# Causal attention's relative-position transfers: shorter rows for the upper 64 partitions, and the triangle filled by GpSimd selects instead of TensorE mask products

## The reference

```python
QEr = jnp.einsum('bhsd,ld->bhsl', q, Er_s)
Srel = _skew(QEr)                 # row s is shifted so that column t holds Er of distance s - t
QK = jnp.einsum('bhsd,bhtd->bhst', q, k)
attn = (QK + Srel) / math.sqrt(dh)
attn = jnp.where(tril, attn, -jnp.inf)
attn = softmax(attn); out = attn @ v
```

## Time and profile before

| | |
|---|---|
| three executions | 1282.5, 1283.88, 1286.7 us |
| the profiled execution | 1286.1 us |
| its span, first to last instruction | 1284.6 us |
| mean granted TensorE clock | 0.91 |
| busy: TensorE, VectorE, ScalarE, GpSimd | 1011.8, 696.2, 647.5, 223.0 us |
| causal attention, first load issued to last score | about 81 to 385 us |

### The profile page before, as it was taken

One profiled execution on the slowest core, in us unless ns is written; L12 is line 12 of the kernel. 1 busy time (PEld: TensorE's weight loads), 2 busy tenths in 40 slices (PEclk: granted clock), 3 DMA queues, 4 the chain that ended last, 5 costly groups with the idle time before them and its releaser, 6 DMA issues. The chain is left out here.

```text
span 1284.6 us, 22764 instructions
## 1 busy us (share of the span) xinstructions
PE 1011.8 (79%) x6434; PEld 632.7 (49%) x6435; DVE 696.2 (54%) x2140; ACT 647.5 (50%) x1346; POOL 223.0 (17%) x531
## 2 busy tenths in 40 slices
PE   5746778788783746999999993355899999997487
PEld 3414444455452425999999992121333333334344
DVE  4735778888887621010101101475766666684597
ACT  2435777777772212333232331143677777763787
POOL 0000000000000360111111112701222222240232
PEclk9865999999996877999999997576999999998799
DMA  7478889999998657665666641345211111110001
GB/s 247 149 258 307 321 329 337 344 341 339 337 324 329 237 180 240 189 214 185 208 196 195 208 147 50 103 157 155 63 47 46 47 44 48 44 38 9 1 29 39
DMA packets 93319, 227.41 MB, mean 177 GB/s; under 512 B 9686, under 2 KB 51766, under 8 KB 87254
## 3 DMA queue, kind: packets, MB, share of 16 engines
q1 hardware_dynamic: 86454, 208.20, 46.5%
q0 software_dynamic: 6816, 18.62, 5.3%
HBM read 143.07 MB, written 83.62 MB: 176 GB/s over the span
## 5 line engine op out<-in xcount | busy, mean ns | idle before, releaser
L684 DVE CUSTOM_DVE_ANT_0 unused<-mpsS,mask_bias 128x512 bf16<-128x512 f32 x256 | 172.0, 691 | 82.8 <-PE mpsS L617 82.7
L711 ACT ACTIVATE mPT<-mpsB 128x512 f32<-128x512 f32 x256 | 152.6, 597 | 80.0 <-PE mpsB L624 73.7
L1358 ACT ACTIVATE hT<-ph,w 128x128 f32<-128x128 f32 x312 | 89.0, 368 | 198.0 <-PE ph L1332 198.0
L464 PE MATMUL psT<-ident,scores 128*128 128x128 f32 x640 | 108.6, 286 | 58.0 <-ACT scores L557 56.1
L1377 DVE TENSOR_TENSOR ys<-py,b 128x256 f32<-128x256 f32 x39 | 16.6, 425 | 249.3 <-PE py L1342 249.3
L512 DVE CUSTOM_DVE_ANT_0 scores<-psS,bias 128x512 f32<-128x512 f32 (+3 forms) x256 | 119.7, 487 | 53.1 <-DMA bias<-rel 45.1
L1332 PE MATMUL ph<-xT,w 128*128 128x128 f32 x1248 | 146.8, 276 | 0.0
L552 ACT COPY stage<-psE 128x512 f32<-128x512 f32 (+1 forms) x192 | 97.5, 510 | 97.6 <-DMA rel<-stage 70.8
L1332 PEld LDWEIGHTS ph<-xT,w 128*128 128x128 f32 x1248 | 143.7, 193 | 0.1
L1342 PE MATMUL py<-w,hT 128*128 x624 | 141.2, 379 | 0.7 <-DVE ys L1377 0.7
L557 ACT ACTIVATE scores<-scores,nm 128x128 f32<-128x128 f32 (+3 forms) x256 | 136.8, 566 | 5.2 <-DVE nm L525 5.2
(11 more groups left out here) (247 smaller groups left out, 1482.5 us busy)
## 6 DMA issues: line engine op xcount, KB each, us to landing
rel<-stage SPq DMA_DIRECT2D x64, 640.0 KB, 6.7
bias<-rel SPq DMA_DIRECT2D x64, 640.0 KB, 7.2
w<-in_w1p SPq DMA_DIRECT2D x39, 1028.0 KB
qk<-packed SPq DMA_DIRECT2D x64, 192.0 KB
mqk<-packed SPq DMA_DIRECT2D x64, 192.0 KB
w<-in_w2p SPq DMA_DIRECT2D x8, 1024.0 KB
slots_in<-zero_row SPq DMA_DIRECT2D x1, 4992.0 KB, 18.2
xs<-slots_in SPq DMA_DIRECT2D x39, 128.0 KB
```

The costliest lines, as they stand in the source:

```text
L464: tr = nc.tensor.transpose(psT[bank][:, to:to + P], scores[slot][:, at:at + P], ident[:, :])
L684: nc.vector.tensor_tensor_reduce(out=unused[:, i, :], in0=psS[i % 2][:, :], in1=mask_bias[:, i, :], scale=1.0, scalar=-3.0e38, op0=ALU.add ...
L711: nc.scalar.activation(PT[r][:, j, :], psB[j % 2][:, :], ACT.Exp, scale=1.0 / 4).then_inc(s_exp, 1)
```

## The change

The columns of `stage` and `rel` are laid out anew: tile 1 at 0, tile 2 at 256, tile 0 at 640, tile 3 at 768, so that two segments of 640 columns (`SEG`) each begin with a tile. The row pitch of `rel` becomes 1281 elements (5124 bytes), and column 1280 of `stage` holds -2^100 from the start. For every head GpSimd runs two `affine_select` instructions on `stage`, each over 2 x 128 columns of 128 rows: of each tile's first 128 columns, row p keeps those from column 127 - p on and gets -2^100 below. After the skew these elements stand above the diagonal of the neighbouring tile, so the mask products are gone. In rows 0 to 63 the first 64 columns of both segments would always be -2^100. They are set once, in DRAM (in the opening) and in `bias`, and are left out of both transfers. So each write and each read becomes two DMAs: rows 64 to 127 whole, and rows 0 to 63 as two pieces of 576 columns (2304 bytes) each.

```diff
+UNIT_AT = [768, 256, 0]
+TRIM = P // 2
+SEG = 640
...
+    REL_P = REL_W + 1
+    rel = [dram(f"rel_{r}", (P, REL_P), F32) for r in range(RING)]
...
@@ SP
-                            sp.wait_ge(s_wr[slot], 16 * (turn + 1))
+                            sp.wait_ge(s_wr[slot], 32 * (turn + 1))
...
-                            skewed = bass.AP(rel[slot].ap().tensor, P - 1, [[REL_W - 1, P], [1, REL_W]])
-                            sp.dma_start(bias[slot][:, :], skewed).then_inc(s_rd[slot], 16)
+                            rel_t = rel[slot].ap().tensor
+                            if isinstance(n, int) and n == -READ:
+                                sp.wait_ge(s_blank_bias, RING)
+                            sp.dma_start(bias[slot][TRIM:P, :], bass.AP(rel_t, P - 1 + TRIM * (REL_P - 1), [[REL_P - 1, P - TRIM], [1, REL_W]])
+                                         ).then_inc(s_rd[slot], 16)
+                            sp.dma_start(bias[slot][0:TRIM, :].rearrange("p (g c) -> p g c", c=SEG)[:, :, 0:SEG - TRIM],
+                                         bass.AP(rel_t, P - 1, [[REL_P - 1, TRIM], [SEG, 2], [1, SEG - TRIM]])).then_inc(s_rd[slot], 16)
...
-                            sp.wait_ge(s_eev, NU * (m + 1))
-                            wait(sp, s_rd[slot], 16 * turn)
-                            sp.dma_start(rel[slot][:, :], stage[slot % 2][:, :]).then_inc(s_wr[slot], 16)
+                            sp.wait_ge(s_cut, 2 * (m + 1))
+                            if isinstance(n, int) and n == -REL:
+                                sp.wait_ge(s_edge, 2)
+                            wait(sp, s_rd[slot], 32 * turn)
+                            sp.dma_start(rel[slot][TRIM:P, :], stage[slot % 2][TRIM:P, :]).then_inc(s_wr[slot], 16)
+                            sp.dma_start(bass.AP(rel[slot].ap().tensor, TRIM, [[REL_P, TRIM], [SEG, 2], [1, SEG - TRIM]]),
+                                         stage[slot % 2][0:TRIM, 0:REL_W].rearrange("p (g c) -> p g c", c=SEG)[:, :, TRIM:SEG]).then_inc(s_wr[slot], 16)
@@ TensorE
-                            nc.tensor.matmul(psS[bank][:, off:off + w], q_k[:, i * P:(i + 1) * P],
-                                             q_k[:, S:S + w], start=True, stop=False)
-
-                            mm = nc.tensor.matmul(psS[bank][:, off + w - P:off + w], identb[:, :], dmask[:, :],
-                                                  start=False, stop=True)
+                            mm = nc.tensor.matmul(psS[bank][:, off:off + w], q_k[:, i * P:(i + 1) * P],
+                                                  q_k[:, S:S + w], start=True, stop=True)
@@ VectorE, ahead of its loop
+                    for rows in stage:
+                        nc.vector.memset(rows[:, REL_W:REL_P], NEG).then_inc(s_edge, 1)
+                    for r in range(RING):
+                        nc.vector.memset(bias[r][0:TRIM, :], NEG).then_inc(s_blank_bias, 1)
@@ GpSimd
-                    pool.wait_ge(vals.s_zero, 3)
+                    keep = dict(base=-(P - 1), channel_multiplier=1, compare_op=ALU.is_ge, fill=nc.gpsimd.to_reg(NEG))
...
+                        if h := stage_of(n, r, it, REL):
+                            m, slot, turn = h
+                            rows = stage[slot % 2]
+                            pool.wait_ge(s_eev, NU * (m + 1))
+                            pool.sem_inc(s_seen_pool, 1)
+                            for first in (rows[:, 0:2 * SEG].rearrange("p (u c) -> p u c", c=SEG)[:, :, 0:P],
+                                          rows[:, 256:1280].rearrange("p (u c) -> p u c", c=512)[:, :, 0:P]):
+                                nc.gpsimd.affine_select(out=first, in_=first, pattern=[[0, 2], [1, P]], **keep).then_inc(s_cut, 1)
+                        if isinstance(n, int) and n == 0:
+                            pool.wait_ge(vals.s_zero, 3)
...
-                    run_heads(pool, 0, NBH - 1, step)
+                    run_heads(pool, -LOAD, NBH - 1, step)
@@ ScalarE
-                                nc.scalar.copy(stage[slot % 2][:, 512 * i:512 * i + WU[i]],
+                                nc.scalar.copy(stage[slot % 2][:, UNIT_AT[i]:UNIT_AT[i] + WU[i]],
@@ opening, SP, between the load of above and the wait on s_es
+                        sp.wait_ge(s_blank, 1)
+                        for r in range(RING):
+                            sp.dma_start(bass.AP(rel[r].ap().tensor, 0, [[REL_P, TRIM], [SEG, 2], [1, TRIM]]),
+                                         blank[:, :, :]).then_inc(s_blank, 16)
+                            sp.dma_start(bass.AP(rel[r].ap().tensor, REL_W - 1, [[REL_P, TRIM], [1, 2]]), blank[:, 0, 0:2]).then_inc(s_blank, 16)
```

More of the change, by code:

```diff
@@ L64, in build @@
     slots_out = dram("slots_out", (SLOT_TILES * P, D), F32)
-    rel = [dram(f"rel_{r}", (P, REL_W), F32) for r in range(RING)]
+    REL_P = REL_W + 1
+    rel = [dram(f"rel_{r}", (P, REL_P), F32) for r in range(RING)]
     with top:
@@ L82, in build @@
         s_const = sem("s_const")
+        s_blank = sem("s_blank")
         s_ctx = [sem(f"s_ctx{i}") for i in range(2)]
@@ L384, in causal_attention @@
             WU = [u[-1][1] + u[-1][2] for u in units]
-            place = {i: (512 * u + off, w) for u, unit in enumerate(units) for i, off, w in unit}
+            place = {i: (UNIT_AT[u] + off, w) for u, unit in enumerate(units) for i, off, w in unit}
             key_place = {j: (512 * u + off, w) for u, unit in enumerate(CAUSAL_KEYS) for j, off, w in unit}
@@ L390, in causal_attention @@
                 qk = [sb(ctx, f"qk{r}", [KP, 2 * S], BF16) for r in range(ROUND)]
-                stage = [sb(ctx, f"stage{r}", [P, REL_W]) for r in range(2)]
+                stage = [sb(ctx, f"stage{r}", [P, REL_P]) for r in range(2)]
                 bias = [sb(ctx, f"bias{r}", [P, REL_W]) for r in range(RING)]
@@ L403, in causal_attention @@
                 s_rd = [sem(f"s_rd{r}") for r in range(RING)]
-                names = ("emm", "eev", "smm", "soft", "nm", "exp", "tmm", "tev", "seen", "seensp")
-                s_emm, s_eev, s_smm, s_soft, s_nm, s_exp, s_tmm, s_tev, s_seen, s_seen_sp = (
+                s_blank_bias = sem("s_blank_bias")
+                names = ("emm", "eev", "smm", "soft", "nm", "exp", "tmm", "tev", "seen", "seensp", "cut", "edge", "seenpool")
+                s_emm, s_eev, s_smm, s_soft, s_nm, s_exp, s_tmm, s_tev, s_seen, s_seen_sp, s_cut, s_edge, s_seen_pool = (
                     sem(f"s_{n}") for n in names)
@@ L502, in step @@
                             m, slot, turn = soft
-                            dve.wait_ge(s_rd[slot], 16 * (turn + 1))
+                            dve.wait_ge(s_rd[slot], 32 * (turn + 1))
                             wait(dve, s_tmm, NU * (m - RING + 1))
@@ L510, in step @@
                                 for i, off, w in unit:
-                                    at = 512 * u + off
+                                    at = UNIT_AT[u] + off
                                     ttr = nc.vector.tensor_tensor_reduce(
@@ L543, in step @@
                         if early and (not isinstance(n, int) or early[0] >= 2):
-                            act.wait_ge(s_wr[(r + REL - 2) % RING], 16 * (it * (ROUND // RING) + (r + REL - 2) // RING + 1))
+                            act.wait_ge(s_wr[(r + REL - 2) % RING], 32 * (it * (ROUND // RING) + (r + REL - 2) // RING + 1))
                         if soft:
@@ L734, in opening @@
                     above = sb(c1, "above", [P, P])
+                    blank = sb(c1, "blank", [TRIM, 2, TRIM])
                     s_er, s_above, s_cc, s_es, s_pick = (sem(f"s_{n}") for n in ("er", "above", "cc", "es", "pick"))
@@ L764, in _ @@
                         sp.wait_ge(s_pick, 16 * PIECES)
+                        sp.wait_ge(s_blank, 16 * 2 * RING + 1)
                         k.stored(sp)
@@ L801, in _ @@
                         nc.vector.memset(zero_row[:, :], 0.0).then_inc(s_cc, 1)
+                        nc.vector.memset(blank[:, :, :], NEG).then_inc(s_blank, 1)
                         nc.vector.memset(V[:, :, :, DH:VW], 1.0).then_inc(s_cc, 1)
```

## The result

The changed kernel takes **1345.8 us** (median of four runs, 1343.4 to 1347.4) and the kernel before, on the same chip, 1284.2: ratio **1.0477**, 95% interval 1.0453 to 1.0501. That is 62 us slower (57 us between the two profiled executions, 1343.4 and 1286.1). The forecast was 3 us faster; the sign is that of rival A, which gave 1361.

The account below looks back on a forecast made before the run. Six DMA engines were taken to bound the stage at 98%. Pace -4.2, mask products at half clock -1.0 and start +1.8 gave -3.4 us: 1280.5 us from the median 1283.9, range 1275 to 1380 (own range 1275 to 1287).

Parts of the forecast that it names:

- rival A: rel transfers touching only 64 partitions run at half rate: 5.8 us a head, some 1361 us, up to 1380; chance 0.33.
- the price of the shorter transfers: rel writes and reads: smaller packets cut the six engines' time to 4.30 us a head, 0.07 to 0.09 less.
- Six engines as the bound: DMA queue: qk loads of 96 rows sit on six engines, which bound the stage at 98%, 4.37 us for 4.47 measured.
- what is late next: Behind the transfers stands the compute loop waiting for TensorE's product, floor 4.34 us; pace taken as 4.39, 4.2 us less.
- This loop keeps its length: Compute loop of TensorE and ScalarE: removing the mask products leaves its 4.34 us unchanged.
- Mask products at pace, nothing: TensorE: their 51.7 us are busy time of an engine that waits anyway, so removing them gains nothing at pace.
- Rival B: Something small eats the gain: odd-pitch rows, selects over 2.1 us, or a later TensorE clock rise; together 0.15, 1285 to 1325.
- The microsecond at half clock: TensorE at 1.2 GHz: without mask products 0.32 us a head over three heads, 1.0 us less (0 to 2).
- Selects: GpSimd, two a head at 0.5 us each (0.3 to 1.5); they delay the write but cost nothing at pace.
- Row pitch: Part of the second rival: writes to 5124-byte rows could cost 10 ns or more a packet, 0 to +5 us.
- SP's issues: SP: two more DMA issues a head at 0.33 us each, 2.1 us of 4.4 in all, hidden by the queue's line.
- Start: Head 0, before the first score: selects, handing over and second issues add 1.8 us (1 to 3).

Follow-up runs that it names:

- before_spread: The kernel before with packed and ErP's rows reordered so each qk load is one run of 96 rows, spread over the engines: 1276.9 us, ratio 0.9915.
- whole: The changed kernel with each rel transfer one DMA of 128 partitions and all 1280 columns again, no trim: 1296.9 us, ratio 1.0082.
- whole_spread: whole with the qk load spread over the engines as one run of 96 rows: 1278.7 us, ratio 0.9938 to the kernel before.
- whole_masks: whole with the three mask products a head put back on TensorE: 1297.4 us, ratio 1.0078 to the kernel before.
- the transfers alone: A program of only SBUF-DRAM transfers, not a changed kernel: 64 partitions 207 to 214 GB/s, whole 387 to 410, odd pitch out 412.
- before_cols: The kernel before with each rel write and read cut into two DMAs by columns, 128 partitions each: 1288.1 us, ratio 1.0020.
- half_writes: The kernel before with rel writes cut into two DMAs by rows and reads into two by columns: 1271.9 us, ratio 1.0060 (another chip).
- before_rows: The kernel before with each rel write and read cut into two DMAs by rows, at full width: 1331.0 us, ratio 1.0339.
- after_untrimmed: The changed kernel without the trim, both row halves at all 1280 columns: 1329.3 us, ratio 1.0515 to the kernel before (another chip).

## Why the prediction was wrong

**The step that failed** is the price of the shorter transfers: "On each of the sixteen engines a write and a read become 4 packets of 5.1 KB and 8 of 2304 bytes each", costed at 197 and 93 ns. The count is right. The prices come from transfers over 96 or 128 partitions. On 64 partitions with sixteen engines bytes go at half the rate (207 to 214 for 398 to 410 GB/s alone), so a packet of the same size takes about twice as long. In the changed kernel the pace came to 5.45 us, where the sum had 4.39. Rival A named this with place, price and point of decision (below 279 GB/s for the transfers of `rel`; measured 1.245 MB / 5.45 us = 228), and was put aside for weak evidence: six engines at 24 bytes per ns each show nothing of sixteen. With no row against it, and a page of the Trainium skill that spoke for it, it should have been the forecast.

**Rival A's own size** was too large, 5.8 us a head for 5.45, and the windows show 264 GB/s, not little over 210. It gave half the rate to both ways. Cut writes by turns keep three quarters of it (301 of 410), and in the kernel they cost 0.6%. Part of the 5.45 comes from the six engines, which A had in its upper bound alone: with the loads spread the pace is 4.89.

**Six engines as the bound:** right. Spread loads take the pace to 4.37 and the waits to TensorE, as the step on what is late next said.

**What is late next:** 4.34 is confirmed by before_spread. "This loop keeps its length" without mask products is off by 0.1 us (4.22 in whole and whole_spread).

**Mask products at pace, nothing:** right in sum by whole and whole_masks (1.0082 and 1.0078), but as two effects that cancel: 0.1 us less in the loop, and more heads at a low clock. Rival B's later rise of the clock did not come: TensorE is first granted full speed for a whole head at about 120 us in the changed kernel and at 126 before. What came is that it falls again. The microsecond at half clock could not be told apart.

**Selects:** their time was right (0.41 for 0.5), and so was the shorter line that takes up the delay, but "hidden" was not quite: 0.3%. **Row pitch** (rival B put it at 0 to +5 us) measured 0.4%, about 5 us; the transfers alone show no such cost, so where it arises in the kernel stays open.

**SP's issues:** forecast at 0.33 us, they take 0.47 and 0.61 in the changed kernel (rows above). before_cols, with as many (0.32 to 0.42 each), loses 0.2%, and half_writes (0.58) 0.6%.

**Start:** +4.1 us at the first score for a forecast 1.8 (1 to 3). 1.4 of it comes before the first write, 2.7 behind it: the first write and read are themselves in halves. before_rows, which has only the halves, stands at 102.02, 3.4 later than before.

**The sum after the fact:** row halves 3.4%, selects and pitch together 0.8% (whole), trim 0 to -0.6% (up to -0.7% by the intervals): 3.6 to 4.2% of 4.8%. The rest, some 8 to 15 us, is not explained by any single part. after_untrimmed against before_rows has it too (5.15% for 3.4 + 0.8). That small delays cost more once transfers are late would fit, but no run tests it.

## What to carry to other kernels

Before a transfer is shortened by leaving out rows, look at which partitions it still touches: cutting `rel` into DMAs over 64 of 128 partitions saved 5% of its bytes here, and such a DMA has half of the rate alone; the stage went from 340 to 264 GB/s. Cut in two by columns, the same transfers kept their rate (334). And look at what splits a DMA over the engines: the gain was not in the large transfers but in a 192 KB load that sat on six engines; laid out as one run of 96 rows it took 0.9% off the whole program.

## What the runs showed of the hardware that was not expected

- Halves by turns recover out (301 of 410 GB/s) but not in (228 of 398).
- A DMA share of 0.96 to 1.03 says nothing of the rate: it stood beside 207, 264, 343 and 410 GB/s. The bytes moved per full share tell it.
- Taking work from TensorE lowered its granted clock and in sum cost no time that the runs can tell: 0.84 or 0.92 at a pace of 5.45 or 5.47. A head at 0.50 is longer all the same, 5.71 us for 4.22 at the least, and the work left out gives 0.1 us a head back.
- Nearly each head of before_spread takes 4.34 to 4.36 us (every eighth 4.52), where before they went from 4.33 to 5.31: loading the engines alike also made the pace even.
